# Two chained attention blocks on one core: another order for the first image, and softmax tiles handed on in halves of 512 queries

## The chip, the core and the metric

The kernel runs on one NeuronCore of a Trainium2 chip. Its engines are TensorE (PE in the profile; the loading of its weights is PEld), VectorE (DVE), ScalarE (ACT), GpSimd (POOL) and SyncE (SP), which only issues DMAs here. Each engine works through its own list of instructions in the order in which the program wrote them, and the engines meet at semaphores. The metric is the device time of one execution in microseconds (us), as the median of several runs; lower is better.

## The reference

Eight images of 256 channels by 1024 pixels pass through two attention blocks. Cut to what is computed:

```
# block 0, for each image x of [256, 1024]
q, k = Wq @ x + bq, Wk @ x + bk          # [32, 1024] each
v    = Wv @ x + bv                       # [256, 1024]
attn = softmax(q.T @ k, axis=-1)         # [1024, 1024]
x    = gamma * (v @ attn.T) + x
# block 1
h    = group_norm(x, 32 groups) * w + b
q, k, v = q_w @ h + q_b, k_w @ h + k_b, v_w @ h + v_b        # [256, 1024] each
attn = softmax(q.T @ k / 16, axis=-1)
x    = x + proj_w @ (v @ attn.T) + proj_b
```

All inputs and outputs are float32.

## The kernel before

**Precision.** Each big product is made of three matmuls. An operand is split into a rounded part (`_hi`) and the rest (`_lo`), and hi by hi, hi by lo and lo by hi are added up (lines 597 to 599). So whatever ScalarE casts into a `_hi` tile, VectorE (or GpSimd) must subtract into a `_lo` tile before the product can run.

**Block 0 of an image** has these pieces. `qk` (two halves of 512 pixels) projects queries and keys, and ScalarE and VectorE copy them out to `q4` and `k4`. `scores` (8 tiles of 128 query rows by 1024 keys, line 607) exist only for the sums of the softmax: VectorE takes the row maximum (line 1067), ScalarE takes the exponent and sums the row (line 844). After eight tiles ScalarE takes the logarithm (line 849), VectorE makes the `shift` of each query (lines 1092 to 1094), TensorE turns it into a row (line 636), and ScalarE copies that to `q4` (line 854). `keys` (8 tiles of 128 keys by 1024 queries, line 617) are the transposed scores with the shift already in them. ScalarE takes their exponent (line 820), which is the finished probability, and rounds it (line 834), VectorE subtracts (line 1084), and TensorE multiplies the tile by the values, twelve matmuls into four banks (half of the queries times half of the channels). `value0` (4 tiles) projects the values.

**Block 1** does the same with 8 `logits` tiles and its own `query` and `value1` projections. The weights of block 1 are first multiplied with each other (`weights`, line 701), and their biases too (`bias`, lines 704 to 718).

**Where results stand.** PSUM holds a `ring` of four slots of 1024 columns. While values are summed, slots 2 and 3 are theirs, and every score, keys, projection and shift tile takes turns in slots 0 and 1. TensorE may write a slot only after the engines have read what stood there before: `wait_read` looks up the reader of the former tenant. The table `PLACE` gives the slots by hand, `HOST` lets a half tile share the slot of another.

**What sets the order.** The order is written out by hand in `first_image`, `second_image` and `turn`, as a list of steps. A step has one keys or logits tile (`tile`), one tile whose values are summed (`values`, two steps behind), and lists of other entries: `early` stands right behind the tile, `sides` between the first `banks_first` banks and the others, `late` at the end. All engines walk through the same list, and each does its own part of each entry: ScalarE its exponent or copy, VectorE its maximum or subtraction. An entry moved in the list moves on all three engines.

**The first image** has nothing beside it: loads, splits, `qk`, values and scores one after the other, while the scores of image 1 (`scores 1,k`) are laced in between its keys tiles. In what follows, `keys 0,4` is the keys tile 4 of image 0, `value0 1,0` the first value tile of image 1, and so on.

## Time and profile before

| | us |
|---|---|
| median of 3 runs | 789.38 |
| lowest and highest | 786.51, 790.51 |
| profiled execution, device time | 785.61 |
| its span in the trace | 783.8 |
| TensorE busy | 774.1 (99%) |
| VectorE busy | 554.7 (71%) |
| ScalarE busy | 470.7 (60%) |
| GpSimd busy | 163.8 (21%) |

The span runs from the first to the last instruction. The mean granted clock of TensorE was 0.998 of full speed. A matmul counts as busy from its start to a modelled end, which overlaps the next one (0.39 us for 512 columns, while the next starts after 0.23). The starts are the sharper measure, and a stall shown as idle before an instruction is some 0.16 us longer when it is read from the starts.

### The profile page before, as it was taken

How to read it: one execution, taken by the hardware profiler on the slowest of the kernel's cores; microseconds unless marked ns; L12 is line 12 of the kernel's file. 1: busy time of each engine (PE TensorE's matmuls, PEld its weight loads, DVE VectorE, ACT ScalarE, POOL GpSimd, SP SyncE). 2: the span in 40 equal slices, each digit the busy share in tenths (PEclk: the TensorE clock that was granted, in tenths of full speed). 3: DMA queues.
4: the chain of work that ended last, by engine and by line, in shares of the span. 5: the costliest groups of instructions: out<-in, count | busy, mean ns of one | idle time of the engine just before them, and what ended most of it. 6: DMA issues, size and time to landing. Idle time of an engine off the chain costs nothing.

```text
span 783.8 us, 9844 instructions
## 1 busy us (share of the span) xinstructions
PE 774.1 (99%) x3816; PEld 647.4 (83%) x3816; DVE 554.7 (71%) x806; ACT 470.7 (60%) x619; POOL 163.8 (21%) x147
## 2 busy tenths in 40 slices
PE   9899999999999999999999999999999999999998
PEld 8678888888888888888888888888888888888886
DVE  5966778787578875788657796677856765476664
ACT  4876566567555775467745586456855566345343
POOL 5730052023100331005110240102310024111120
PEclk9999999999999999999999999999999999999999
DMA  6010010002000110001100011000100000000101
GB/s 189 0 55 1 1 54 1 1 23 86 1 1 1 55 54 1 1 1 54 55 1 1 0 56 54 1 1 0 54 1 2 0 33 22 1 0 1 54 1 54
DMA packets 10365, 18.98 MB, mean 24 GB/s; under 512 B 2128, under 2 KB 3920, under 8 KB 10320
## 3 DMA queue, kind: packets, MB, share of 16 engines
q1 hardware_dynamic: 10320, 18.36, 6.8%
q8 instruction: 30, 0.49, 0.3%
q14 instruction: 15, 0.12, 0.1%
HBM read 9.97 MB, written 8.39 MB: 23 GB/s over the span
## 4 chain that ended last, share of the span: by engine, by line
PE 95%; ACT 2%; DVE 2%; issue 0%; POOL 0%; ACTq 0%; DVEq 0%; POOLq 0%
PE ring L597 29%; PE ring L599 28%; PE ring L598 28%; PE ring L617 4%; PE ring L607 3%; PE ring L594 1%; ACT ring L844 1%; ACT pt_hi L834 1%; ACT prob L820 1%; PE ring L636 1%; DVE neg_max L1067 0%; DVE res L1120 0%; DVE pt_lo L1084 0%; PE ring L691 0%; PE ring L716 0%
## 5 line engine op out<-in xcount | busy, mean ns | idle before, releaser
L597 PE MATMUL ring<-pt_hi,v_hi 128*128 128x512 f32 x480 | 189.4, 395 | 0.0
L599 PE MATMUL ring<-pt_hi,v_lo 128*128 128x512 f32 x480 | 188.5, 393 | 0.0
L598 PE MATMUL ring<-pt_lo,v_hi 128*128 128x512 f32 x480 | 188.3, 392 | 0.0
L823 ACT ACTIVATE prob<-ring,neg_max 128x1024 f32<-128x1024 f32 x64 | 71.5, 1118 | 155.1 <-DVE neg_max L1070 155.1
L1069 DVE TENSOR_REDUCE neg_raw<-ring 128x1 f32<-128x1024 f32 x64 | 78.2, 1222 | 58.0 <-PE ring L599 57.9
L504 POOL TENSOR_TENSOR v_lo<-v_f,v_hi 128x512 fp32r<-128x512 f32 x28 | 37.7, 1347 | 385.1 <-ACT v_hi L861 385.1
L1084 DVE TENSOR_TENSOR pt_lo<-prob,pt_hi 128x1024 fp32r<-128x1024 f32 x64 | 81.8, 1278 | 37.5 <-ACT pt_hi L834 37.3
L599 PEld LDWEIGHTS ring<-pt_hi,v_lo 128*128 128x128 f32 x480 | 90.3, 188 | 19.9
L597 PEld LDWEIGHTS ring<-pt_hi,v_hi 128*128 128x128 f32 x480 | 90.5, 188 | 18.4 <-issue 0.4
L598 PEld LDWEIGHTS ring<-pt_lo,v_hi 128*128 128x128 f32 x480 | 90.6, 189 | 18.2
L1067 DVE TENSOR_REDUCE neg_max<-ring 128x1 f32<-128x1024 f32 x64 | 77.7, 1223 | 35.4 <-PE ring L607 35.3
L844 ACT ACTIVATE ring<-ring,neg_max 128x1024 f32<-128x1024 f32 x64 | 69.4, 1084 | 39.9 <-DVE neg_max L1067 39.8
L1087 DVE SCALAR_TENSOR_TENSOR pt_lo<-prob,row_inv,pt_hi 128x1024 fp32r<-128x1024 f32 x64 | 83.1, 1298 | 8.6 <-ACT pt_hi L837 8.4
L597 PE MATMUL ring<-h_hi,query_hi 128*128 128x512 f32 x224 | 88.0, 393 | 0.0
L598 PE MATMUL ring<-h_lo,query_hi 128*128 128x512 f32 x224 | 87.5, 391 | 0.0
L599 PE MATMUL ring<-h_hi,query_lo 128*128 128x512 f32 x224 | 87.5, 391 | 0.0
L820 ACT ACTIVATE prob<-ring 128x1024 f32<-128x1024 f32 x64 | 65.5, 1024 | 36.4 <-PE ring L617 36.2
L837 ACT ACTIVATE pt_hi<-prob,row_inv 128x1024 fp32r<-128x1024 f32 x64 | 73.7, 1152 | 9.6 <-DVE row_inv L1076 9.3
L834 ACT CAST pt_hi<-prob 128x1024 fp32r<-128x1024 f32 x64 | 67.3, 1051 | 5.3
L599 PEld LDWEIGHTS ring<-h_hi,query_lo 128*128 128x128 f32 x224 | 42.0, 188 | 8.9
L597 PEld LDWEIGHTS ring<-h_hi,query_hi 128*128 128x128 f32 x224 | 42.1, 188 | 8.8 <-ACT prob L823 0.2
L598 PEld LDWEIGHTS ring<-h_lo,query_hi 128*128 128x128 f32 x224 | 42.1, 188 | 8.6
(167 smaller groups left out, 1346.8 us busy)
## 6 DMA issues: line engine op xcount, KB each, us to landing
out_y<-res SPq DMA_DIRECT2D x32, 256.0 KB, 2.2
x_in<-in_x SPq DMA_DIRECT2D x7, 1024.0 KB, 4.9
x_in<-in_x SPq DMA_DIRECT2D x2, 512.0 KB, 5.2
h_f<-in_wv_t SPq DMA_DIRECT2D x1, 256.0 KB, 4.4
res<-in_wq SPq DMA_DIRECT2D x1, 256.0 KB, 6.8
res<-in_wk SPq DMA_DIRECT2D x1, 256.0 KB, 7.1
res<-in_wv SPq DMA_DIRECT2D x1, 256.0 KB, 7.6
res<-in_wp_t SPq DMA_DIRECT2D x1, 256.0 KB, 7.1
```

What stands on the lines that cost most here:

```text
L597: mm(out, w_hi, m_hi, start=first, stop=False)
L598: mm(out, w_hi, m_lo, start=False, stop=False)
L599: return mm(out, w_lo, m_hi, start=False, stop=last)
L820: activation(prob[:, p % PROBS], ring[:, slot], ACT.Exp).then_inc(S["keys_exp"], 1)
L823: activation(prob[:, p % PROBS], ring[:, slot], ACT.Exp, bias=neg_max[:, k % 2:k % 2 + 1], accum_out=row_sum[:, k % 2:k % 2 + 1]).then_inc ...
L834: copy(pt_hi[p % PT][:], prob[:, p % PROBS]).then_inc(S["p_hi"], 1)
L837: activation(pt_hi[p % PT][:], prob[:, p % PROBS], ACT.Identity, scale=row_inv[:, k % 2:k % 2 + 1]).then_inc(S["p_hi"], 1)
L844: activation(ring[:, slot], ring[:, slot], ACT.Exp, bias=neg_max0[:, k:k + 1], accum_out=row_sum0[:, k:k + 1]).then_inc(S["scores_exp"], 1)
L1067: V.tensor_reduce(neg_max0[:, k:k + 1], src, AX_X, ALU.max, negate=True).then_inc(S["scores_max"], 1)
L1069: link(V.tensor_reduce(neg_raw[:, k % 2:k % 2 + 1], src, AX_X, ALU.max, negate=True))
L1084: V.tensor_tensor(lo[:], src, hi[:].bitcast(F32), ALU.subtract).then_inc(S["p_split"], 1)
L1087: V.scalar_tensor_tensor(lo[:], src, row_inv[:, k % 2:k % 2 + 1], hi[:].bitcast(F32), ALU.mult, ALU.subtract).then_inc(S["p_split"], 1)
```

## The change

Only the first image, the start of image 1 and the keys tiles of all images are touched.

- **Loads.** The first half of image 0 is loaded first, in two pieces of 128 channels, and then the query and key weights. The second half and the small biases follow in exchanged order. The first splits go piece by piece: four casts of 128x512 on ScalarE and four subtractions on VectorE in place of two and two of 128x1024. TensorE's opening run of matmuls on a tile of ones is 18 long in place of 30.
- **Queries and keys of image 0.** For the second half ScalarE, not VectorE, makes the first key part, and the first four score tiles wait for the first half of the queries only.
- **Order of image 0.** Before the scores stands one value tile in place of two. Value tile 1 and the four weight products stand between the score tiles, value tiles 2 and 3 and both `qk` halves of image 1 around the shift and the first keys tiles. `scores 1,0` to `scores 1,7` move later: they stand at the end of steps 3, 4 and 5 and within steps 6, 7 and 8, where they stood right behind the keys tiles of steps 2 to 7.
- **Halves.** ScalarE makes each keys tile as exponent, cast, exponent, cast of 512 columns each, VectorE subtracts half by half, and the first two banks of the values wait for the first half only.
- **Bias products.** The same products in another order, the wide ones in pieces of 128 columns.

The core of the diff:

```diff
-PLACE = {("qk", 1, 0): 2, ("value0", 0, 2): 3, ("bias", 0, 0): 3}
+PLACE = {("qk", 0, 0): 1, ("qk", 0, 1): 0, ("value0", 0, 0): 3, ("value0", 0, 2): 0, ("qk", 1, 0): 2, ("shift", 0, 0): 1,
+         ("keys", 0, 0): 1, ("keys", 0, 1): 3, ("bias", 0, 0): 3}
+PLACE.update({("scores", 0, k): (2, 1, 0)[k % 3] for k in range(TILES)})
 PLACE.update({("keys", 0, k): 1 for k in range(2, TILES)})
-PLACE.update({("scores", 1, k): 0 for k in range(7)})
+PLACE.update({("scores", 1, k): int(k in (5, 7)) for k in range(TILES)})
 PLACE.update({("value0", 1, 0): 1, ("value0", 1, 1): 1, ("value0", 1, 2): 0})
...
-    for k in range(6):
-        steps[k + 2].early = tiles("scores", 1, (k,))
+    steps[0].late = tiles("qk", 1, (1,))
+    steps[1].late = tiles("value0", 0, (3,))
+    for k, s in enumerate((3, 4, 5)):
+        steps[s].late = tiles("scores", 1, (k,))
     steps[4].sides = tiles("value0", 1, (0,))
-    steps[6].sides = tiles("value0", 1, (1,))
+    steps[6].sides = tiles("value0", 1, (1,)) + tiles("scores", 1, (3,))
     steps[6].x_lo_end = 2, 0
-    s8, s9, s10 = Step(None, (0, 0, 6)), Step(None, (0, 0, 7)), Step(("keys", 1, 1))
+    steps[7].sides, steps[7].late = tiles("scores", 1, (4,)), tiles("scores", 1, (5,))
+    s8, s9, s10 = Step(None, (0, 0, 6), 3), Step(None, (0, 0, 7)), Step(("keys", 1, 1))
+    s8.early_behind = True
     s8.early = tiles("scores", 1, (6, 7))
...
+                    ("x0_loaded0", ((x_in[0][:, 0, half_cols[0]], x_v[0][:, 0, half_cols[0]]),)),
+                    ("x0_loaded1", ((x_in[0][:, 1, half_cols[0]], x_v[0][:, 1, half_cols[0]]),)),
                     ("wqk_loaded", ((wqk_f, by_tile(wqk_t)),)),
-                    ("x0_loaded", ((x_in[0][:, :, half_cols[0]], x_v[0][:, :, half_cols[0]]),)),
+                    ("bqk_loaded", ((bqk_s[:], bqk), (bk0_s[:], bk0))),
...
-                if 0 in banks:
-                    wait("p_split", p + 1)
                 for b in banks:
                     half, ct = bank_of[b]
+                    if layer == 0 and b == 0:
+                        wait("half_split", i * TILES + k + 1)
+                    elif b == (0 if layer else CT):
+                        wait("p_split", p + 1)
...
-            keep_busy(ring[:, 3], 30)
+            keep_busy(ring[:, 3], 18)
...
+            def keys_probs(tile):
...
+                for half, cols in enumerate(half_cols):
+                    part = prob[:, p % PROBS][:, cols]
+                    done = ("keys_half", "keys_exp")[half]
+                    activation(part, ring[:, slot][:, cols], ACT.Exp).then_inc(S[done], 1)
+                    if half == 0 and p >= PT:
+                        name, n = values_done(TILE_OF[p - PT])
+                        act.wait_ge(S[name], n)
+                    act.wait_ge(S[done], i * TILES + k + 1)
+                    copy(pt_hi[p % PT][:, cols], part).then_inc(S[("half_hi", "p_hi")[half]], 1)
```

How this moves the instructions is shown at step 4 of image 0, on two engines. TensorE before, from the keys tile on: L617 is `keys 0,4`, L607 is `scores 1,2`, L597 to L599 on `pt` are half of the values of tile 2, and L597 on `wv0` begins `value0 1,0`, whose slot `keys 0,4` held.

```order
L617 MATMUL ring<-q4_0,k4_0 128x512 [waits keys_exp]
L617 MATMUL ring<-q4_0,k4_0 128x512
L607 MATMUL ring<-k4_1,q4_1 128x512 [waits scores_exp]
L607 MATMUL ring<-k4_1,q4_1 128x512
L597 MATMUL ring<-pt_hi2,v0_hi 128x512 [waits p_split,value0_first]
L598 MATMUL ring<-pt_lo2,v0_hi 128x512
L599 MATMUL ring<-pt_hi2,v0_lo 128x512
L597 MATMUL ring<-pt_hi2,v0_hi 128x512
L598 MATMUL ring<-pt_lo2,v0_hi 128x512
L599 MATMUL ring<-pt_hi2,v0_lo 128x512
L597 MATMUL ring<-wv0_hi,h_hi 128x256 [waits keys_exp]
```

TensorE after, at the same place. L616 is the scores line there, L626 the keys line, L601 to L603 the three matmuls:

```order
L616 MATMUL ring<-k4_1,q4_1 128x512 [waits qk_split,key_hi,value0_kept]
L616 MATMUL ring<-k4_1,q4_1 128x512
L626 MATMUL ring<-q4_0,k4_0 128x512 [waits keys_exp]
L626 MATMUL ring<-q4_0,k4_0 128x512
L601 MATMUL ring<-pt_hi2,v0_hi 128x512 [waits half_split,value0_first]
L602 MATMUL ring<-pt_lo2,v0_hi 128x512
L603 MATMUL ring<-pt_hi2,v0_lo 128x512
L601 MATMUL ring<-pt_hi2,v0_hi 128x512
L602 MATMUL ring<-pt_lo2,v0_hi 128x512
L603 MATMUL ring<-pt_hi2,v0_lo 128x512
L601 MATMUL ring<-wv0_hi,h_hi 128x256 [waits keys_exp]
```

The score tile (`scores 1,0`) now stands just ahead of `keys 0,4`, not behind it, and the value tile waits for the same exponent (`keys_exp`) as before.

ScalarE before, around the same step: L820 and L834 are the exponent and the cast of a keys tile, L844 is the exponent of a score tile, L876 the cast of a value tile.

```order
L834 CAST pt_hi3<-prob 128x1024 [waits keys_exp]
L844 ACTIVATE ring,row_sum0<-ring,neg_max0 128x1024 [waits scores_max]
L820 ACTIVATE prob<-ring 128x1024 [waits ring_ready,p_split]
L834 CAST pt_hi0<-prob 128x1024 [waits keys_exp,tile_done]
L844 ACTIVATE ring,row_sum0<-ring,neg_max0 128x1024 [waits scores_max]
L876 CAST v0_hi<-ring 128x512 [waits ring_ready]
```

ScalarE after: L864 and L869 are exponent and cast of half a keys tile, L875 is the exponent of a score tile, L907 the cast of a value tile.

```order
L869 CAST pt_hi3<-prob 128x512 [waits keys_exp]
L875 ACTIVATE ring,row_sum0<-ring,neg_max0 128x1024 [waits scores_max]
L864 ACTIVATE prob<-ring 128x512 [waits ring_ready,p_split]
L869 CAST pt_hi0<-prob 128x512 [waits keys_half,tile_done]
L864 ACTIVATE prob<-ring 128x512
L869 CAST pt_hi0<-prob 128x512 [waits keys_exp]
L907 CAST v0_hi<-ring 128x512 [waits ring_ready]
```

Between the keys tiles 3 and 4 there stands one score tile's exponent in both. Before it is that of `scores 1,1`, which TensorE writes one step before `keys 0,4`, and now that of `scores 1,0`, which TensorE writes directly ahead of it.

## Rows read from the trace of the kernel before

**Rows 1.** The page: busy us, share, count; and TensorE's busy tenths in 40 slices.

```profile
PE 774.1 (99%) x3816; PEld 647.4 (83%) x3816; DVE 554.7 (71%) x806; ACT 470.7 (60%) x619; POOL 163.8 (21%) x147
...
PE   9899999999999999999999999999999999999998
```

**Rows 2.** Windows: the start-up, and the stretch at a lower granted clock.

```profile
9.12:69.03 59.91, 54.40 (x274) 43.07 (x272) 45.19 (x50) 44.12 (x64) 30.27 (x28) 1.00 0.15 49
75.70:79.10 3.40, 3.40 (x9) 2.63 (x9) 3.30 (x10) 2.23 (x3) 0.00 (x0) 0.50 0.00 0
```

**Rows 3.** Timeline of TensorE: start, length, line, names, count, idle before.

```profile
0.98 8.39 PE L594 MATMUL ring<-ones 128*128 128x128 f32 x60 [0.98 <-POOL unit L544]
9.12 0.48 PE L597 MATMUL ring<-x_hi,wqk_hi 128*128 128x512 f32 x1
...
12.01 0.28 PE L597 MATMUL ring<-wv_hi,x_hi 128*128 128x256 f32 x1
12.12 0.28 PE L598 MATMUL ring<-wv_lo,x_hi 128*128 128x256 f32 x1
...
15.74 1.62 PE L607 MATMUL ring<-k,q 96*128 96x512 f32 x6 [0.75 <-DVE q L1039]
...
28.52 0.64 PE L636 MATMUL ring<-ident_r,shift_pair 128*2 128x128 f32 x8 [0.81 <-DVE shift_pair L1094]
...
35.56 0.40 PE L597 MATMUL ring<-pt_hi,v_hi 128*128 128x512 f32 x1
35.79 0.40 PE L598 MATMUL ring<-pt_lo,v_hi 128*128 128x512 f32 x1
...
40.38 0.73 PE L607 MATMUL ring<-k,q 96*128 96x512 f32 x2 [1.46 <-ACT ring L844]
...
46.00 0.28 PE L597 MATMUL ring<-wv_hi,h_hi 128*128 128x256 f32 x1
```

**Rows 4.** Timeline of TensorE, later.

```profile
55.08 0.28 PE L597 MATMUL ring<-wv_hi,h_hi 128*128 128x256 f32 x1
...
69.03 0.65 PE L636 MATMUL ring<-ident_r,shift_pair 128*2 128x128 f32 x8
```

**Rows 5.** Timeline of VectorE, same columns.

```profile
7.06 1.22 DVE L962 TENSOR_TENSOR x_lo<-x_in,x_hi 128x1024 fp32r<-128x1024 f32 x1 [3.38 <-ACT x_hi L805]
...
14.74 0.74 DVE L1039 SCALAR_TENSOR_TENSOR q<-ring,bqk_s,q 32x512 fp32r<-32x512 f32 x1
16.48 6.88 DVE L1067 TENSOR_REDUCE neg_max<-ring 128x1 f32<-128x1024 f32 x6 [0.99 <-PE ring L607]
...
34.36 0.68 DVE L1046 TENSOR_SCALAR h_f<-ring 128x512 f32<-128x512 f32 x1
...
36.05 1.90 DVE L1084 TENSOR_TENSOR pt_lo<-prob,pt_hi 128x1024 fp32r<-128x1024 f32 x1 [0.42 <-ACT pt_hi L834]
```

**Rows 6.** Timeline of ScalarE, same columns.

```profile
5.99 1.04 ACT L805 CAST x_hi<-x_in 128x1024 fp32r<-128x1024 f32 x1 [3.98 <-DMA x_in<-in_x]
...
10.87 0.68 ACT L886 ACTIVATE q<-ring,bqk_s 64x512 fp32r<-64x512 f32 x1 [2.33 <-PE ring L599]
...
17.73 1.09 ACT L844 ACTIVATE ring<-ring,neg_max 128x1024 f32<-128x1024 f32 x1 [2.12 <-DVE neg_max L1067]
18.75 0.19 ACT L844 ACTIVATION_READ_ACCUMULATOR ring<-ring,neg_max 128x1 f32 x1
...
27.56 0.21 ACT L849 ACTIVATE log_sum<-row_sum 128x8 f32<-128x8 f32 x1
...
31.08 1.02 ACT L820 ACTIVATE prob<-ring 128x1024 f32<-128x1024 f32 x1 [0.18 <-PE ring L617]
32.14 1.04 ACT L834 CAST pt_hi<-prob 128x1024 fp32r<-128x1024 f32 x1
```

**Rows 7.** Timeline of GpSimd, same columns.

```profile
8.77 1.50 POOL L512 CAST wv_hi<-h_f 128x512 fp32r<-128x512 f32 x1 [5.77 <-DMA ident_s<-in_ident]
10.35 1.28 POOL L513 TENSOR_TENSOR wv_lo<-h_f,wv_hi 128x512 fp32r<-128x512 f32 x1
```

More of the change, by code:

```diff
@@ L706, in bias_products @@
                 value_b_ps, rowk_ps, query_b_ps = bias_places(slot)
-                for o in range(CT):
-                    mm(value_b_ps[:, 0:C], bv_rows[:, o], wp_f[:, o], start=o == 0, stop=o == CT - 1)
                 for j in range(2):
@@ L713, in bias_products @@
                 for ct in range(CT):
+                    cols = slice(ct * P, (ct + 1) * P)
+                    for o in range(CT):
+                        mm(value_b_ps[:, cols], bv_rows[:, o], wp_f[:, o, cols], start=o == 0, stop=o == CT - 1)
                     for out, w, b in ((rowk_ps, wq_f, bk_s), (query_b_ps, wk_f, bq_s)):
@@ L782, in _ @@
                 for entry in now.early + front if now.early_in_front else front + now.early:
-                    fill(entry)
+                    if not (now.early_behind and entry in now.early):
+                        fill(entry)
                 if now.values:
                     values(now.values, range(now.banks_first))
+                if now.early_behind:
+                    for entry in now.early:
+                        fill(entry)
                 for entry in now.sides:
@@ L796, in _, with first_split_x @@
             nc.scalar.preload_act_table_set("natural_log_exp_and_others")
+            def first_split_x():
+                for half in range(HALVES):
+                    for ct in range(CT):
+                        if half == 0:
+                            act.wait_ge(S[("x0_loaded0", "x0_loaded1")[ct]], 16)
+                        else:
+                            act.wait_ge(x_loaded[0], x_loads(0))
+                        copy(x_hi[:, ct, half_cols[half]], x_in[0][:, ct, half_cols[half]]).then_inc(S["x0_hi"], 1)
             def split_x(i):
+                act.wait_ge(x_loaded[i % 2], x_loads(i))
                 for half in range(HALVES):
                     cols = half_cols[half]
-                    if i == 0 and half == 0:
-                        act.wait_ge(S["x0_loaded"], 16)
-                    else:
-                        act.wait_ge(x_loaded[i % 2], x_loads(i))
                     copy(x_hi[:, :, cols], x_in[i % 2][:, :, cols]).then_inc(S["x_hi"], 1)
@@ L887, in query_part, with first_key_part @@
                            bias=bqk_s[0:64]).then_inc(S["qk_hi"], 1)
+            def first_key_part(entry):
+                act.wait_ge(S["ring_ready"], RING_NO[entry] + 1)
+                activation(k4[0][0:32, half_cols[entry[2]]], half_place(entry)[64:96], ACT.Identity,
+                           bias=bqk_s[64:96]).then_inc(S["key_first"], 1)
             def key_part(entry):
@@ L895, in opening @@
                 log_sums(0)
-                for m in range(2):
-                    query_part(("qk", 1, m))
                 shift_rows(("shift", 0, 0))
+                query_part(("qk", 1, 0))
                 key_part(("qk", 1, 0))
@@ L910, in follow @@
                     project_hi(entry)
-            split_x(0)
+            first_split_x()
             for now in STEPS:
@@ L957, in _, with first_split_x @@
             scale = C ** -0.5
+            def first_split_x(half):
+                cols = half_cols[half]
+                for ct in range(CT):
+                    dve.wait_ge(S["x0_hi"], CT * half + ct + 1)
+                    last = V.tensor_tensor(x_lo[:, ct, cols], x_in[0][:, ct, cols], x_hi[:, ct, cols].bitcast(F32),
+                                           ALU.subtract)
+                last.then_inc(S["x_split"], 1)
             def split_x(i, half):
                 cols = half_cols[half]
-                dve.wait_ge(S["x_hi"], 2 * i + half + 1)
+                dve.wait_ge(S["x_hi"], 2 * (i - 1) + half + 1)
                 V.tensor_tensor(x_lo[:, :, cols], x_in[i % 2][:, :, cols], x_hi[:, :, cols].bitcast(F32),
@@ L973, in first_weights @@
             def first_weights():
+                first_split_x(0)
                 dve.wait_ge(S["wqk_loaded"], 16)
                 split(wqk_hi[:], wqk_lo[:], wqk_f).then_inc(S["layer0_split"], 1)
-                for half in range(HALVES):
-                    split_x(0, half)
+                first_split_x(1)
             def biases(slot):
@@ L1015, in project_lo @@
                     last.then_inc(S["query_split"], 1)
+                if entry == ("value0", 0, 3):
+                    keep_values()
                 if kind == "value0" and i:
@@ L1056, in opening @@
                 shifts(0)
-                for m in range(2):
-                    key_part(("qk", 1, m))
-                for m in range(2):
-                    query_part(("qk", 1, m))
+                take_weights()
+                key_part(("qk", 1, 0))
+                query_part(("qk", 1, 0))
             def row_max(entry):
```

109 lines of the change are left out of this document (58 added, 51 removed).

## Prediction

> **What bounds the kernel now.** I read the page first. TensorE is busy for 774.1 of 783.8 us, and only the first slices and the last are not full [rows 1]. So from about 69 us on only TensorE's own work counts, and a change of order can win or lose only ahead of that. The window from the first projection to the shift of image 1 shows 54.40 busy of 59.91 us [rows 2]. Counted from the starts it is emptier: 512 columns start every 0.23 us (35.56 to 35.79) and 256 every 0.12 us [rows 3], which makes the matmuls of that window 51.1 us (24 score and keys tiles at 0.47, 4 `qk` halves and 7 value0 tiles at 1.41, 7.5 value sums at 2.73, and 3.9 for the weight products and the shift) and leaves 8.8 us of stalls. Ahead of it lie 9.12 us of start. The window at 75.70 shows a granted clock of 0.50 for 3.40 us [rows 2], 1.7 us lost. These three (9.12, 8.8, 1.7) are all that there is to win.
>
> Marks by which I compare: `value0 1,0` starts at 46.00, `value0 1,1` at 55.08 and the shift of image 1 at 69.03 [rows 3, 4]. At the third, the same work is done before and after.
>
> **Prices.** A score or keys tile takes 0.47 on TensorE and reaches its reader 0.74 after its start (15.74 to 16.48) [rows 3, 5]. A row maximum is 1.22 (1.15 each in a row), then ScalarE's exponent 1.09 plus its sum of 0.19, 1.21 until the slot is free, 1.13 for the next [rows 5, 6]. Exponent and cast of a whole keys tile start 1.06 apart and take 1.02 and 1.04 [rows 6]. No row shows a half on ScalarE. By length alone it would be 0.51; the 512-wide bias activation took 0.68 [rows 6]. I take 0.59 for each half and 0.62 and 0.53 between starts, nearer to the first since the whole tile has one such start in it: 1.74 from the first exponent to the end of the second, 2.30 for all four, where the whole tile takes about 2.05. So ScalarE gets 0.25 us more per tile, 16 us over 64 tiles, off the path: it is 60% busy. VectorE's halves cost 0.6 each (34.36: 0.68 long) [rows 5].
>
> **1. Start: about 2 us won, then 0.** Before, the first projection starts at 9.12, when the run of ones ends (0.98 + 8.39) [rows 3], though the first `x_lo` is ready at 7.06 + 1.22 = 8.28 [rows 5]. Now 18 passes are over at about 6.4. The same 640 KB have to land, which they had by 5.99 [rows 6]; then the weight split (about 0.75) comes last, so the projection starts at 7.2. Its second half waits for casts and subtractions of the second load (two of each, until about 9.55) and ends at 11.1. But `value0 0,0` needs GpSimd's split of its weights, which ended at 10.35 + 1.28 = 11.63 [rows 7] and whose load is now issued one place later: 12.0, as before (12.01). The lead is gone there. It comes back because one value tile, not two, stands ahead of the scores: TensorE reaches them at 13.4, VectorE ends its last query part at 14.36 (15.48 before) and takes the first maximum at 14.4, not 16.48.
>
> **2. Scores of image 0: a lead of 2.1 us.** Eight exponents at 1.13 and one copy of 0.59 (`value0 0,1`, now among them) follow from 15.65: the last ends at 25.4, the logarithm starts at 25.45 (27.56 before [rows 6]), the shift on TensorE at 26.4 (28.52). The weight products and one value tile fit into TensorE's waits.
>
> **3. From the shift to the first values: the lead is spent.** Before, the `qk` halves of image 1 were done by the shift. Now ScalarE idles 1.5 us for the shift (26.4 + 0.68 = 27.1), copies it until 28.1, waits for `qk 1,0`, copies that (two at 0.71) and starts `keys 0,0` at 30.1 (31.08 before [rows 6]). Behind it stand `qk 1,1` (1.42) and two more tiles (4.6): their last cast starts at 37.9 and ends at 38.5, about where before (38.0). The value banks take the slot of the `qk` tiles of image 1, whose last query part VectorE ends at 35.45: values start at 35.65, before at 35.56 [rows 3]. There `scores 1,0` was done, now it isn't. The next tile has no stall, where 40.38 showed 1.46 (1.62 by starts) [rows 3]. Net: `scores 1,0` at 41.6, `keys 0,4` at 42.05, half of values 2 until 43.9. Before, that point was 46.00 with two score tiles more done (0.94): 1.2 us ahead.
>
> **4. `value0 1,0`: what decides.** It takes the slot of `keys 0,4`, so it waits for that tile's exponent, before and now. What changed is what ScalarE has in front: the exponent of `scores 1,0`, which TensorE writes directly ahead. From `scores 1,0` at 41.6: 0.74 to the maximum, 1.25 to the exponent, 1.13 to `keys 0,4`, 1.74 to its end: 46.5. TensorE is there at 43.9 and stands 2.6 us. All engines work in list order, so nothing can pass. Before, the score tile was written a step earlier.
>
> **5. `value0 1,1`: again, longer.** `scores 1,1` starts at 46.5 + 1.41 + 1.37 = 49.3. Then 0.74, 1.25, 1.13: `keys 0,5` on ScalarE at 52.4, its last cast done 2.39 later (54.8). VectorE must subtract that before it takes the maximum of `scores 1,2` (0.65: 55.45). Then 1.25 and 1.13, `keys 0,6` at 57.8, and 1.74: 59.6. TensorE's own work from 49.3 is only 6.0 us (two score and two keys tiles, one and a half value sums), so 4.4 us are lost, 0.8 ahead of `keys 0,6` and 3.6 ahead of `value0 1,1`, which starts at 59.6, not 55.08 [rows 4], with three score tiles done, not five.
>
> **6. Until the shift.** Five score tiles are left where there were three. `scores 1,3` to `1,7` stand between 61.0 and 72.0; VectorE's subtraction of `keys 0,7` (until 68.0) is ahead of the maximum of `scores 1,4`, and the last four go one by one through maximum and exponent: TensorE waits 0.35, 1.05, 0.55 and 0.35. Log at 74.85, shift at 75.8 against 69.03 [rows 4].
>
> **Sum.** 7.2 of start + 51.1 of work + stalls of 1.1 and 0.9 (start), 2.5 (scores), 0.6 (shift), 3.0 (first values), 2.6, 0.8, 3.6 and 2.3 = 75.7 to 75.8; before 9.12 + 51.1 + 8.8 = 69.0. So +6.8. Behind it TensorE is full, the halves have room, and I leave the lower clock as it is. The profiled execution took 785.61 us: 792.4. It lies 3.8 under the median of 789.38, so on the scale of the medians 796.2, which I give as 796.
>
> **Bounds.** Ten halves stand on the chains of 4 and 5: at 0.51 each they give 0.8 back, at 0.68 they cost 0.9. The start may be 0.6 off either way by the loads. VectorE and GpSimd: a subtraction of 1.22 elsewhere took 1.90 [rows 5] while GpSimd worked; GpSimd now works for the values 2 and 3 while `keys 0,3` is subtracted, 0 to 0.7 more. The reordered bias products hold the same 24 one-column matmuls, in a row before. The lower clock stands right behind them [rows 2]; it may stay (0), go (-1.7), or also follow the new stalls (+1.7 each).
>
> The Trainium skill, "TensorE: Matmul & The Clock Gate", section "HAM oscillation — how this bites in real kernels", says that idle gaps between bursts of matmuls drop the engine to half clock. The trace agrees that it is not only a full stop that counts (0.50 at 75.70, behind narrow matmuls without a gap [rows 2]), yet the 1.46 us at 40.38 brought none. By that rule the stalls of 2.6 and 3.6 us would cost up to 1.7 us each, and the sum would be 795.8 on the profile's scale in place of 792.4.
>
> **Rivals.**
> - *The clock falls at the new stalls*, by the mechanism just priced: half speed for as long as at 75.70, behind one or both: +8.5 to +10.2, 798 to 800. For it: 3.6 us is over twice any stall now. Against: it needs TensorE to be the bound just then. 0.15.
> - *Smaller stalls, no measurable change.* Halves at 0.51 (-0.8), a start 0.6 sooner, the lower clock gone (-1.7): +3.7, 793. 0.17.
> - *Faster.* ScalarE's exponent of `scores 1,k` is not in the way, because the keys exponent gets free earlier than I read: the place is `value0 1,0`, and it decides if the exponent of `keys 0,4` ends before 43.9. Then the 1.2 us lead stands, the two chains cost nothing, and with the lower clock gone it is -1.2 - 1.7: 786.5; if ScalarE's idle time of section 3 is avoided too, 2 us more: 784.5. For it: the lead of 2.1 at the shift. Against: the list order leaves no way round. 0.10.
> - *The forecast*, +5 to +8: 0.58.
>
> A change under 0.5% (3.9 us) can't be told from none. Slower 0.72, same 0.19, faster 0.09. The range of 788 to 801 leaves out the faster rival (about 1 in 10) and little at the top, since it holds the lower clock at both stalls.
>
> **What would show it.** Right: TensorE idle 2 to 3 us ahead of `value0 1,0` and 3 to 4 ahead of `value0 1,1`, both released by ScalarE's exponent of a keys tile; shift of image 0 near 26.4 and of image 1 near 75.8; nothing new behind that. Wrong: no idle of over 1.5 us at those two tiles, or a first value sum well ahead of 35, which would mean that section 3 spends less than I think, or stalls in later images, which would mean that ScalarE's extra 16 us have no room.

## The result

The changed kernel takes 813.24 us (811.13 to 815.18, four runs), the kernel before 788.64 us (786.51 to 790.51, four runs; the table ahead of the prediction has 789.38 from three of them). The ratio is 1.0312, with a 95% interval of 1.0274 to 1.035: 3.1% slower. The forecast was 796 with a range of 788 to 801. The direction was right and the size was not: +24.6 us between the medians, +27.4 us of span in the profiled executions (783.8 to 811.2), where +6.8 was forecast.

### The profile page after: what moved, and what is told of

Same layout as the page of the kernel before. It is cut to its first block, busy times and chain, and to the rows that moved or that the text cites. A ratio compares the mean times of both kernels' runs of the same rounds, so it can differ in the third digit from the quotient of the medians.

```text
span 811.2 us, 10013 instructions
## 1 busy us (share of the span) xinstructions
PE 788.2 (97%) x3796; PEld 650.8 (80%) x3796; DVE 564.6 (70%) x871; ACT 488.5 (60%) x750; POOL 161.4 (20%) x147
## 4 chain that ended last, share of the span: by engine, by line
PE 80%; ACT 12%; DVE 4%; issue 2%; DMA 1%; SPq 0%; ACTq 0%; DVEq 0%
PE ring L601 26%; PE ring L603 24%; PE ring L602 24%; ACT prob L864 5%; ACT pt_hi L869 4%; PE ring L626 3%; PE ring L616 2%; ACT h_hi L832 1%; DVE neg_max L1119 1%; ACT ring L875 1%; DMA x_in<-in_x 1%; PE ring L645 0%; DVE pt_lo L1140 0%; DVE h_lo L1016 0%; PE ring L710 0%
## 5 line engine op out<-in xcount | busy, mean ns | idle before, releaser
L601 PE MATMUL ring<-pt_hi,v_hi 128*128 128x512 f32 x480 | 190.6, 397 | 2.9 <-DVE q L1092 2.9
L603 PE MATMUL ring<-pt_hi,v_lo 128*128 128x512 f32 x480 | 189.4, 395 | 0.0
L1140 DVE TENSOR_TENSOR pt_lo<-prob,pt_hi 128x512 fp32r<-128x512 f32 x128 | 91.8, 734 | 36.1 <-ACT pt_hi L869 35.6
L601 PEld LDWEIGHTS ring<-pt_hi,v_hi 128*128 128x128 f32 x480 | 91.3, 190 | 22.0 <-issue 3.7
L603 PEld LDWEIGHTS ring<-pt_hi,v_lo 128*128 128x128 f32 x480 | 91.0, 190 | 20.0
L875 ACT ACTIVATE ring<-ring,neg_max 128x1024 f32<-128x1024 f32 x64 | 69.5, 1086 | 49.7 <-DVE neg_max L1119 49.6
L864 ACT ACTIVATE prob<-ring 128x512 f32<-128x512 f32 x128 | 75.9, 593 | 32.1 <-PE ring L626 31.4
L601 PE MATMUL ring<-h_hi,query_hi 128*128 128x512 f32 x224 | 88.0, 393 | 0.0
L603 PE MATMUL ring<-h_hi,query_lo 128*128 128x512 f32 x224 | 87.5, 391 | 0.0
L869 ACT CAST pt_hi<-prob 128x512 fp32r<-128x512 f32 x128 | 79.5, 621 | 7.4
L603 PEld LDWEIGHTS ring<-h_hi,query_lo 128*128 128x128 f32 x224 | 42.1, 188 | 8.9
L601 PEld LDWEIGHTS ring<-h_hi,query_hi 128*128 128x128 f32 x224 | 42.1, 188 | 8.9 <-DVE v_lo L1067 0.2
```

Source lines behind the costliest of these rows:

```text
L601: mm(out, w_hi, m_hi, start=first, stop=False)
L603: return mm(out, w_lo, m_hi, start=False, stop=last)
L864: activation(part, ring[:, slot][:, cols], ACT.Exp).then_inc(S[done], 1)
L869: copy(pt_hi[p % PT][:, cols], part).then_inc(S[("half_hi", "p_hi")[half]], 1)
L875: activation(ring[:, slot], ring[:, slot], ACT.Exp, bias=neg_max0[:, k:k + 1], accum_out=row_sum0[:, k:k + 1]).then_inc(S["scores_exp"], 1)
L1140: V.tensor_tensor(lo[:, cols], src[:, cols], hi[:, cols].bitcast(F32), ALU.subtract).then_inc(S[("half_split", "p_split")[half]], 1)
```

## The profile after

The page: busy us, share of the span and count; TensorE's busy tenths and the granted clock in 40 slices; the new groups of half keys tiles (exponent, cast, subtraction: busy, mean ns of one, idle before).

```profile
PE 788.2 (97%) x3796; PEld 650.8 (80%) x3796; DVE 564.6 (70%) x871; ACT 488.5 (60%) x750; POOL 161.4 (20%) x147
...
PE   8887999999999999999999999999999999999998
...
PEclk9899899999999999999999999999999999999999
...
L864 ACT ACTIVATE prob<-ring 128x512 f32<-128x512 f32 x128 | 75.9, 593 | 32.1 <-PE ring L626 31.4
L869 ACT CAST pt_hi<-prob 128x512 fp32r<-128x512 f32 x128 | 79.5, 621 | 7.4
L1140 DVE TENSOR_TENSOR pt_lo<-prob,pt_hi 128x512 fp32r<-128x512 f32 x128 | 91.8, 734 | 36.1 <-ACT pt_hi L869 35.6
```

ScalarE has 17.8 us more than in [rows 1], about the 16 that were forecast, and is still at 60%. TensorE has 14 us more of busy time in 20 fewer instructions. Part of that is a lower clock: the mean granted clock fell from 0.998 to 0.987. It is not a matter of one execution: the four runs show 0.983 to 0.989, and no run of the kernel before in the experiments below shows less than 0.993.

TensorE's timeline at the marks of the prediction (start, length, line, names, count, idle before):

```profile
0.98 7.15 PE L598 MATMUL ring<-ones 128*128 128x128 f32 x36 [0.98 <-POOL unit L547]
7.88 0.48 PE L601 MATMUL ring<-x_hi,wqk_hi 128*128 128x512 f32 x1
...
14.19 1.87 PE L616 MATMUL ring<-k,q 96*128 96x512 f32 x6
...
28.64 0.64 PE L645 MATMUL ring<-ident_r,shift_pair 128*2 128x128 f32 x8 [0.36 <-DVE shift_pair L1152]
...
37.88 0.77 PE L601 MATMUL ring<-pt_hi,v_hi 128*128 128x512 f32 x1 [2.93 <-DVE q L1092]
...
50.30 0.39 PE L601 MATMUL ring<-wv_hi,h_hi 128*128 128x256 f32 x1 [2.40 <-ACT prob L864]
...
59.63 0.73 PE L626 MATMUL ring<-q,k 98*128 98x512 f32 x2 [0.57 <-ACT prob L864]
...
65.07 0.58 PE L601 MATMUL ring<-wv_hi,h_hi 128*128 128x256 f32 x1 [3.33 <-ACT prob L864]
...
82.56 0.64 PE L645 MATMUL ring<-ident_r,shift_pair 128*2 128x128 f32 x8
...
86.09 1.20 PE L626 MATMUL ring<-q,k 98*128 98x512 f32 x4 [1.44 <-DVE v_lo L1067]
```

Read the brackets first. The long stalls that were forecast are there with their size, once the 0.16 us are added by which a bracket is short of the starts: 2.40 ahead of `value0 1,0` (2.6 forecast), 0.57 and 3.33 ahead of `keys 0,6` and `value0 1,1` (0.8 and 3.6). Yet the marks run away from the forecast ones, and the windows show why (columns: us, then busy of TensorE, weight load, VectorE, ScalarE, GpSimd with counts, granted clock, DMA share, GB/s):

```profile
9.12:82.56 73.44, 60.16 (x266) 47.01 (x265) 45.88 (x58) 46.99 (x82) 28.89 (x28) 0.91 0.13 45
20.66:24.07 3.41, 3.41 (x9) 2.67 (x9) 2.12 (x3) 3.14 (x6) 3.25 (x5) 0.50 0.02 5
37.73:41.14 3.41, 3.26 (x8) 2.62 (x9) 3.41 (x5) 2.79 (x5) 0.92 (x1) 0.50 0.00 0
51.40:54.80 3.40, 3.40 (x13) 2.82 (x12) 0.92 (x2) 0.59 (x1) 1.51 (x2) 0.50 0.36 142
65.05:68.45 3.40, 3.38 (x14) 3.28 (x15) 0.89 (x2) 1.04 (x2) 0.00 (x0) 0.50 0.00 0
88.92:95.75 6.83, 6.83 (x26) 6.06 (x26) 4.03 (x12) 4.86 (x9) 0.00 (x0) 0.50 0.00 0
```

Four stretches at half clock ahead of the shift of image 1 where there was none [rows 2], and one of 6.83 us after it in place of 3.40. The first of the four can't be put down to the change. Three kernels below keep the old order of image 0 (halves alone, exponents first on the kernel before, bias products), and the profile of each has such a stretch at 22 to 23 us and its shift of image 0 at 30.6 to 30.8, not at 28.52; that of the kernel before happens to have none. The one of halves alone, same columns:

```profile
23.17:26.58 3.41, 3.41 (x15) 3.12 (x14) 1.57 (x3) 2.44 (x6) 0.00 (x0) 0.50 0.00 0
```

| mark | forecast | measured | late by | stretch in between |
|---|---|---|---|---|
| first projection | 7.2 | 7.88 | 0.7 | the run of ones lasts 7.15, not about 5.4 |
| first scores | 13.4 | 14.19 | 0.8 | |
| shift of image 0 | 26.4 | 28.64 | 2.2 | 20.66 |
| first values | 35.65 | 37.88 | 2.2 | |
| `value0 1,0` | 46.5 | 50.30 | 3.8 | 37.73 |
| `value0 1,1` | 59.6 | 65.07 | 5.5 | 51.40 |
| shift of image 1 | 75.8 | 82.56 | 6.8 | 65.05 |

From mark to mark with a stretch in between, the lateness grows by 1.3 to 1.7 us. In all that makes +13.5 us up to the shift of image 1 (82.56 against 69.03 [rows 4]), and 13.9 are still missing. The weight loads of TensorE show where most of them are. Waits of the weight load (engine, line, releaser: us in total, times, longest) from 100 to 700 us, the kernel before:

```profile
PEld ring L597 <- issue: 0.4, 1, 0.4
PEld ring L597 <- ACT prob L823: 0.2, 1, 0.2
```

and the changed one:

```profile
PEld ring L601 <- ACT prob L864: 13.4, 25, 0.6
PEld ring L601 <- DVE v_lo L1067: 2.0, 2, 1.8
```

Twenty-five times TensorE waits for the exponent of a keys tile: five times in each of five images, ahead of two query, two `value1` and one `qk` projection. One of them in the timeline of all engines, same columns as above:

```profile
209.26 0.60 ACT L864 ACTIVATE prob<-ring 128x512 f32<-128x512 f32 x1 [1.21 <-PE ring L626]
...
209.95 0.62 ACT L869 CAST pt_hi<-prob 128x512 fp32r<-128x512 f32 x1
...
210.48 0.59 ACT L864 ACTIVATE prob<-ring 128x512 f32<-128x512 f32 x1
210.60 0.39 PE L603 MATMUL ring<-pt_hi,v_lo 128*128 128x512 f32 x1
...
211.12 0.19 PEld L601 LDWEIGHTS ring<-h_hi,wqq_hi 128*128 128x128 f32 x1 [0.55 <-ACT prob L864]
211.12 0.50 PE L601 MATMUL ring<-h_hi,wqq_hi 128*128 128x512 f32 x1
```

The same place in the kernel before:

```profile
190.26 1.03 ACT L820 ACTIVATE prob<-ring 128x1024 f32<-128x1024 f32 x1 [1.22 <-PE ring L617]
...
191.62 0.39 PE L599 MATMUL ring<-pt_hi,v_lo 128*128 128x512 f32 x1
191.63 0.19 PEld L597 LDWEIGHTS ring<-h_hi,wqq_hi 128*128 128x128 f32 x1
191.85 0.40 PE L597 MATMUL ring<-h_hi,wqq_hi 128*128 128x512 f32 x1
```

The query projection takes the slot of a keys tile, and has to wait for the end of its exponent. Before, that slot was free 1.03 us after the exponent's start (191.29), 0.34 ahead of the weight load at 191.63. (In the trace of before this room is 0.34 at the 20 places with query and `value1` projections and 0.62 at the five with `qk`.) Now the cast of the first half stands between the two exponents, the slot is free after 1.81 (210.48 + 0.59), and TensorE's next matmul starts 0.52 after the last one (210.60 to 211.12) where 0.23 is the usual step: some 0.3 lost here. (The bracket of 0.55 counts from the end of the last weight load.) Add up, over the starts of all matmuls from 100 to 700 us, what goes beyond 0.23 us behind 512 columns, 0.12 behind 256 or 258 and 0.06 behind fewer: it grows from 6.1 to 17.2 us. Of these 11.1 us some 8 lie in the 25 places, 0.33 at each with the step behind it, and 1.5 at one wait of a query projection for VectorE:

```profile
126.54 0.50 PE L601 MATMUL ring<-h_hi,wqq_hi 128*128 128x512 f32 x1 [1.31 <-DVE v_lo L1067]
```

The sum: 13.5 up to the shift of image 1, 1.4 ahead of `keys 1,0` at 86.09, 1.7 for the longer half clock at 88.92, 11.1 in the later images: 27.7 where 27.4 was measured.

## Experiments

Two theories for the cost behind the shift: **slot** (the second exponent of each keys tile ends later, so its slot is given back later) and, as its rival, **load** (ScalarE and VectorE have 18 and 10 us more to do). For the first image: **order** (the score tiles of image 1 stand in the wrong place) and **clock** (the new stalls bring the half clock). Runs of one round share the runs of the kernel before: 786.84, 787.06 and 786.91 us.

### Whole tiles

The changed kernel, with each keys tile as one exponent, one cast, one subtraction again (ScalarE's part; VectorE's subtraction and the waits are put back too).

```diff
-                for half, cols in enumerate(half_cols):
...
-                    activation(part, ring[:, slot][:, cols], ACT.Exp).then_inc(S[done], 1)
...
-                    copy(pt_hi[p % PT][:, cols], part).then_inc(S[("half_hi", "p_hi")[half]], 1)
+                activation(prob[:, p % PROBS], ring[:, slot], ACT.Exp).then_inc(S["keys_exp"], 1)
...
+                copy(pt_hi[p % PT][:], prob[:, p % PROBS]).then_inc(S["p_hi"], 1)
```

> The changed kernel with whole keys tiles again: one exponent, one cast, one subtraction of 1024 columns, the values wait for the whole tile. Theory A (the second half's exponent frees the tile's slot about 0.7 us later than the whole exponent did, which stops TensorE some 25 times for 0.4 us in the later images, about 10 us): 799 to 803 us against 813.2, and TensorE stands nowhere behind 130 us. Theory B (the later images are slower because of the new slots or of the state in which the first image leaves them): 811 to 814. Both: the stalls ahead of value0 1,0 and value0 1,1 stay, 0.7 us shorter each.

Measured: 801.63 us, ratio 1.0182 [1.0153, 1.0212]. The 25 waits are gone, and the loss by starts from 100 to 700 us is 7.9. The stalls of the first image stay, though not both 0.7 shorter, as was expected: one has gone from 2.40 to 1.76, the other from 3.33 to 3.59.

```profile
48.33 0.38 PE L601 MATMUL ring<-wv_hi,h_hi 128*128 128x256 f32 x1 [1.76 <-ACT prob L859]
...
61.04 0.58 PE L601 MATMUL ring<-wv_hi,h_hi 128*128 128x256 f32 x1 [3.59 <-ACT prob L859]
```

So all of the change but the halves costs 14.8 us, and the long stall ahead of `value0 1,1` does not come from the halves. Part of the 14.8 is clock. This profile has 17.1 us of half clock, some 8.5 us lost, where that of the kernel before has 3.4 and 1.7. Two of its three stretches:

```profile
60.77:64.18 3.41, 3.14 (x13) 3.06 (x14) 1.22 (x1) 1.44 (x3) 0.00 (x0) 0.50 0.00 0
84.66:94.90 10.24, 10.24 (x42) 9.47 (x42) 5.74 (x11) 4.68 (x5) 0.00 (x0) 0.50 0.00 0
```

The first goes with the stall of 3.59. Behind the stall of 1.76 no half clock was granted.

### Halves alone

The same edit the other way: the kernel before, with halves.

```diff
-                    activation(prob[:, p % PROBS], ring[:, slot], ACT.Exp).then_inc(S["keys_exp"], 1)
+                    for half, cols in enumerate(half_cols):
...
+                        activation(part, ring[:, slot][:, cols], ACT.Exp).then_inc(S[done], 1)
...
+                        copy(pt_hi[p % PT][:, cols], part).then_inc(S[("half_hi", "p_hi")[half]], 1)
...
-                    copy(pt_hi[p % PT][:], prob[:, p % PROBS]).then_inc(S["p_hi"], 1)
```

> The kernel before with the halves alone: exponent, cast, exponent, cast, two subtractions, the first two banks wait for the first half. Theory A: 798 to 800 us (788.6 and about 10), with the stalls ahead of query, value1 and qk tiles of later images. Theory B: 788 to 790.

Measured: 799.41 us, 1.0146 [1.0117, 1.0176]. Its shift of image 1 comes at 73.05, 4.0 later than before. Of that 2.3 are there at the shift of image 0 (30.82), behind the half clock from 23.17. The run of the bias products meets that too, without any halves (30.80). The weight load shows the row of the changed kernel again:

```profile
PEld ring L597 <- ACT prob L825: 13.4, 25, 0.6
```

### Halves in another order

The changed kernel, with exponent, exponent, cast, cast in place of exponent, cast, exponent, cast. The number of operations and their lengths are the same, so this one tells slot from load.

```diff
                 for half, cols in enumerate(half_cols):
...
-                    copy(pt_hi[p % PT][:, cols], part).then_inc(S[("half_hi", "p_hi")[half]], 1)
+                    activation(prob[:, p % PROBS][:, cols], ring[:, slot][:, cols],
+                               ACT.Exp).then_inc(S[("keys_half", "keys_exp")[half]], 1)
...
+                for half, cols in enumerate(half_cols):
...
+                    copy(pt_hi[p % PT][:, cols],
+                         prob[:, p % PROBS][:, cols]).then_inc(S[("half_hi", "p_hi")[half]], 1)
```

> The changed kernel, ScalarE's four half operations in the order exponent, exponent, cast, cast, so as many operations as in the changed kernel, but the slot is free 0.6 us sooner. Theory A: 802 to 805 us, the recurring stalls are gone or under 0.1 us. Theory C (what costs in the later images is ScalarE's 0.25 us more per tile, its fixed cost): 812 to 814, nothing changes.

Measured: 799.58 us, 1.016 [1.0129, 1.019], some 2 us under what was expected. The loss by starts from 100 to 700 us is back at 6.7, against 6.1 in the kernel before, and the wait of 1.31 at 126.54 is gone too. ScalarE's timeline at the place shown above:

```profile
209.46 1.09 ACT L862 ACTIVATE prob<-ring 128x512 f32<-128x512 f32 x2 [1.22 <-PE ring L626]
210.44 1.14 ACT L869 CAST pt_hi<-prob 128x512 fp32r<-128x512 f32 x2
```

The slot is free 1.09 after the start, not 1.81. The edit also moves the wait for the buffer of the cast behind both exponents, but at the place shown above the first cast began 0.09 after its exponent, so it waited for nothing. With ScalarE's and VectorE's extra work in place, almost the whole cost in the later images is gone: load is refuted, slot is shown. The two long stalls of the first image stay (2.65 and 3.44).

The same order of halves (the + side of this diff) on the kernel before, with nothing else changed:

> The kernel before with halves in the order exponent, exponent, cast, cast. By theory A (slot release) the 25 recurring stalls of the other order of halves don't appear: 786 to 788 us, within 0.3% of before. If ScalarE's extra 0.25 us per tile costs something by itself: 790 or more.

Measured: 788.42 us (12 runs) against 787.06, 1.0017 [1.0, 1.0033]. The halves as such are almost free, and bring nothing.

### Scores where they were

The changed kernel, with `scores 1,k` right behind the keys tiles of steps 2 to 7 again (cut; the parts come in another order than in the kernel).

```diff
-    for k, s in enumerate((3, 4, 5)):
-        steps[s].late = tiles("scores", 1, (k,))
+    for k in range(6):
+        steps[k + 2].early = tiles("scores", 1, (k,))
...
-    s8, s9, s10 = Step(None, (0, 0, 6), 3), Step(None, (0, 0, 7)), Step(("keys", 1, 1))
-    s8.early_behind = True
+    s8, s9, s10 = Step(None, (0, 0, 6)), Step(None, (0, 0, 7)), Step(("keys", 1, 1))
...
-    s9.sides = tiles("value0", 1, (2,)) + tiles("shift", 1, (0,))
+    s8.late = tiles("value0", 1, (2,))
+    s9.sides = tiles("shift", 1, (0,))
...
-PLACE.update({("scores", 1, k): int(k in (5, 7)) for k in range(TILES)})
+PLACE.update({("scores", 1, k): 0 for k in range(7)})
```

Steps 8 and 9 are put back as well, with `value0 1,2` in step 8.

> The changed kernel, halves included, with the scores of image 1 where they stood before (right behind the keys tiles of steps 2 to 7, in slot 0). Theory A: the stalls of 2.4 and 3.3 us ahead of value0 1,0 and 1,1 shrink to under 1 us, and at least three of the six stretches at half clock go: 799 to 803 us. Theory D (the loss in the first 90 us lies in the new order of image 0 itself, loads, weight products and qk): above 806.

Measured: 801.96 us, 1.0185 [1.0154, 1.0215]. Both stalls ahead of value0 tiles are gone, and the shift of image 1 comes at 72.66. In their place stands one that I had not counted:

```profile
37.66 1.19 PE L615 MATMUL ring<-k,q 96*128 96x512 f32 x2 [5.32 <-DVE x L1105]
```

`scores 1,0` takes slot 0, which `value0 0,2` holds until VectorE has copied it, and VectorE does that after the subtraction of a keys tile. So the scores could not simply stay where they were: value tiles 2 and 3 had been moved ahead of them. The 25 waits of the halves are there too (13.3, 25 times).

Both undone in the changed kernel (the diffs of the first and of this experiment together):

> The changed kernel with both suspects undone: whole tiles, and the scores of image 1 where they stood before. If the two losses add up (halves about 12 us, score order about 12 us), this is within 3 us of before: 787 to 790, with the one stall of about 5 us ahead of scores 1,0 that the run with the early scores showed. If a third part of the change costs by itself (loads, order of image 0): above 792.

Measured: 789.49 us, 1.004 [1.0022, 1.0058], with the same stall (5.4). Against the kernel before: halves alone +12.6, the rest of the change alone +14.8, both +26.4 (813.24 against 786.84, not of one round), the new loads and the new start of image 0 with neither +2.6.

### The bias products

The kernel before with the new order of the bias products, since the half clock stands right behind them.

```diff
-                for o in range(CT):
-                    mm(value_b_ps[:, 0:C], bv_rows[:, o], wp_f[:, o], start=o == 0, stop=o == CT - 1)
...
+                    cols = slice(ct * P, (ct + 1) * P)
+                    for o in range(CT):
+                        mm(value_b_ps[:, cols], bv_rows[:, o], wp_f[:, o, cols], start=o == 0, stop=o == CT - 1)
```

> The kernel before with the bias products alone in the order of the changed kernel. If the new order keeps the clock up, the stretch at half clock at about 75 us goes and the time falls by up to 1.7 us (785.1 against 786.8). If the order is nothing to the clock: the stretch stays behind the bias products in most executions, no change. If it makes it worse: one or two stretches, up to 1.7 us slower.

Measured: 787.27 us (10 runs), 1.0005 [0.9985, 1.0025]. Half clock is still granted for 3.4 us there, from 77.7. So this part of the change shows no effect on the time. The stretch is no fixed price of these products: the profiles of both kernels with halves and the old order of image 0 have the old products and full clock there (1.00 in both from 70 to 85 us).

### The stalls filled

The changed kernel, with six passes over the tile of ones ahead of `value0 1,0` and of `value0 1,1`, once the exponent of the score tile is done. TensorE would have stood there anyway.

```diff
                 before = BEFORE[entry]
+                if entry in (("value0", 1, 0), ("value0", 1, 1)):
+                    wait("scores_exp", TILES + 1 + 2 * m)
+                    keep_busy(ring[:, 0], 6)
```

> The changed kernel, and in the two long stalls (ahead of value0 1,0 and 1,1) TensorE runs 6 passes on the tile of ones (1.3 us each time) once the exponent of the score tile in slot 0 is read, so that the stalls stay as long but TensorE idles 1.3 us less in each. If the idle time in them is what lowers the clock (51 and 65 us): those two stretches go and the kernel gets 2 to 3.4 us faster than 813.2, 810 to 811. If the clock falls for another cause: 813 to 814 and stretches at half clock at the same places.

Measured: 812.67 us, 1.032 [1.0293, 1.0347]: no gain that can be told from none. Two windows, same columns as above:

```profile
9.12:80.16 71.04, 60.55 (x290) 47.09 (x289) 46.88 (x58) 46.65 (x81) 28.95 (x28) 0.95 0.13 43
85.40:95.60 10.20, 10.20 (x42) 9.43 (x42) 5.96 (x14) 6.09 (x11) 0.00 (x0) 0.50 0.00 0
```

The stretches at 51.40 and 65.05 are gone (0.95 in place of 0.91), and the shift of image 1 comes 2.4 us sooner, at 80.16. That these two stretches come from the stalls does not rest on this one execution. In the three profiles that have the stalls, half clock began at most 0.3 us ahead of and 1.1 us behind the end of each one of 2.40, 2.65, 3.33, 3.44 and 3.59 us (changed kernel, exponents first, whole tiles), and not at the one of 1.76 or at the two filled ones. But the stretch at the bias products is now 10.20 long, 1.7 us more lost, and so the total missed the expectation. Nothing shows that the filling made it longer: with whole tiles, and nothing filled, it is 10.24 long.

### Towards a better kernel

**Mixed.** The changed kernel with the exponents first, `scores 1,0` to `1,4` right behind the keys tiles of steps 3 to 7, and `1,5` late in step 7.

```diff
-    for k, s in enumerate((3, 4, 5)):
-        steps[s].late = tiles("scores", 1, (k,))
+    for k in range(5):
+        steps[k + 3].early = tiles("scores", 1, (k,))
...
-    steps[6].sides = tiles("value0", 1, (1,)) + tiles("scores", 1, (3,))
+    steps[6].sides = tiles("value0", 1, (1,))
...
-    steps[7].sides, steps[7].late = tiles("scores", 1, (4,)), tiles("scores", 1, (5,))
+    steps[7].late = tiles("scores", 1, (5,))
```

> The changed kernel's order of image 0, halves in the order exponent, exponent, cast, cast, and scores 1,0 to 1,4 right behind the keys tiles of steps 3 to 7 (scores 1,5 to 1,7 as in the changed kernel). By my theory no long stall ahead of value0 1,0 and 1,1 (under 0.5 us), no recurring ones, and of the lead at the shift of image 0 (28.64 against 28.52 in the changed kernel with a clock fall, 26.4 without) something is kept: 785 to 790 us. If the new order of image 0 costs by itself: above 793.

Measured: 790.95 us (784.77 to 792.24, 12 runs), 1.0031 [1.001, 1.0053], just above the range that was expected. The profiled execution was one of the two fastest (784.85, granted clock 0.999) and had full clock from 7.1 to 781 us. It is not the usual one: seven of the twelve runs show 0.988 to 0.991 and took 790.8 to 792.2 us.

```profile
26.66 0.64 PE L645 MATMUL ring<-ident_r,shift_pair 128*2 128x128 f32 x8 [0.41 <-DVE shift_pair L1153]
...
35.82 0.47 PE L601 MATMUL ring<-pt_hi,v_hi 128*128 128x512 f32 x1 [2.85 <-DVE q L1093]
```

```profile
9.12:68.28 59.16, 53.62 (x266) 42.00 (x266) 46.61 (x58) 45.21 (x82) 31.66 (x28) 1.00 0.15 53
```

This is the test of the prediction's ledger at full clock, up to the first values, where the two kernels have the same order: its 26.4 and 35.65 are measured as 26.66 and 35.82. It also shows a stall of 2.85 us with no half clock behind it, and a shift of image 1 at 68.28, 0.75 ahead of the kernel before.

**Opened.** The same, with both `qk` halves of image 1 copied ahead of `keys 0,0`, `scores 1,5` in the sides of step 7 and `value0 1,2` late in step 8.

```diff
-    opening.late = tiles("shift", 0, (0,)) + tiles("qk", 1, (0,))
+    opening.late = tiles("shift", 0, (0,)) + tiles("qk", 1, (0, 1))
...
-    steps[0].late = tiles("qk", 1, (1,))
...
-    steps[7].late = tiles("scores", 1, (5,))
-    s8, s9, s10 = Step(None, (0, 0, 6), 3), Step(None, (0, 0, 7)), Step(("keys", 1, 1))
+    steps[7].sides = tiles("scores", 1, (5,))
+    s8, s9, s10 = Step(None, (0, 0, 6)), Step(None, (0, 0, 7)), Step(("keys", 1, 1))
...
-    s9.sides = tiles("value0", 1, (2,)) + tiles("shift", 1, (0,))
+    s8.late = tiles("value0", 1, (2,))
+    s9.sides = tiles("shift", 1, (0,))
```

> The mixed version again (order of image 0 as changed, halves as exponent, exponent, cast, cast, scores 1,0 to 1,4 behind their keys tiles), and both qk halves of image 1 copied out before the first keys tile's cast is subtracted, scores 1,5 within step 7, value0 1,2 at the end of step 8. The stalls of 2.9 us ahead of the first value sum and of 1.4 us ahead of keys 1,0 shrink by 1.5 us and 1.4 us: 783 to 787 us, faster than before by 0.3% or nothing. If the clock decides (it fell in some executions of the mixed version): two groups of times, as in 784.8 and 791.

Measured: 785.67 us (782.75 to 788.21, 12 runs), 0.9985 [0.9969, 1.0001]. The stall of 2.85 ahead of the first values has become one of 0.7, and the one of 1.4 ahead of `keys 1,0` one of 0.2. In this profile there is a new one at the start, where the second half of the projection waits for its splits:

```profile
PE ring L601 <- DVE x_lo L1003: 2.8, 1, 2.8
```

**Thirty passes.** The same with 30 opening passes in place of 18.

```diff
-            keep_busy(ring[:, 3], 18)
+            keep_busy(ring[:, 3], 30)
```

> The same with the opening run of 30 passes, not 18. If TensorE's idle time between the opening run and the first projections is what lets the clock fall later in the first 25 us: fewer slow executions and a narrower spread than m3_open, median at or under it. If not: the same spread, and up to 1 us slower for the later start.

Measured: 785.77 us (783.48 to 788.11, 12 runs), 0.998 [0.9962, 0.9998]. The 30 passes make no difference that can be told from none (785.67 with 18). The spread is 4.6 us against 5.5, and the times still lie in two groups, six of 783.5 to 784.2 with a clock of 1.0 and six of 787.3 to 788.1 with 0.993 to 0.995, so what was hoped of the clock is not shown. The stalls of 2 us and more are gone, as the largest waits of TensorE show:

```profile
PE ring L616 <- ACT ring L876: 1.8, 4, 0.6
PE ring L598 <- POOL unit L547: 1.0, 1, 1.0
PE ring L601 <- DVE pt_lo L1143: 0.7, 1, 0.7
```

It is the only variant whose interval lies below 1, by 0.2%, which is next to nothing, and it lies 27 us under the changed kernel.

## Why the prediction was wrong

**Start (1): right in kind.** The run of ones lasted 7.15, not about 5.4, so the projection began at 7.88 and not 7.2. Full clock was granted only from about 7.0 us on in that execution, so 18 passes took longer than I counted. (In the kernel before it was from 4.0 on.) By 12.54 GpSimd's split of the weights set the end, as forecast, though at 12.0.

**Scores of image 0 and first values (2, 3): right at full clock.** The lead of 2.1 us at the shift was there in the mixed kernel (26.66) and was spent by the first values, as forecast. In the changed kernel half clock from 20.66, between the weight products, made TensorE late for two maxima and took the lead before the shift (28.64). The kernels with the old order of image 0 lose 2.1 to 2.3 us the same way in their profiles, so against them the lead was there. I read the marks of before from an execution without this stretch, and did not ask how other executions look.

**`value0 1,0`, `value0 1,1` (4, 5): right.** Place, releaser and size, 2.56 and 0.73 + 3.49 by the starts against 2.6 and 0.8 + 3.6. The half lengths taken between the bounds (0.59, 0.62) are those measured. With whole tiles the stalls are 1.76 and 3.59: they are of the order, and the halves have only a part in the first. And with the scores moved back they give way to 5.32 us elsewhere, which the prediction had no need to see but a repair had.

**Until the shift (6): in kind.** Of the four waits that were forecast (2.3 us) two are there, 0.79 and 0.40 at 77.21 and 78.34, 1.5 us by the starts.

**Clock: the first failed step.** "I leave the lower clock as it is" was wrong by four stretches ahead of the shift (5 to 6 us of the 6.8 by which the marks are late) and 1.7 at the bias products. Some 3 us of it are the two behind the long stalls, which follow the idle time, as the stalls of five sizes and the fill run show. The rival had that mechanism at 0.15 and +1.7 each, with the right price and too little chance: the stall of 1.46 at 40.38, which brought no half clock [rows 3], was no evidence about stalls of 2.4 to 3.3. I had read the Trainium skill, "TensorE: Matmul & The Clock Gate", section "HAM oscillation — how this bites in real kernels", for the rule that idle gaps between bursts drop the engine to half clock. The trace agrees in kind, with 0.50 behind gaps of 2.40 and 3.33 us, though both are shorter than the gaps that the page warns of. The rule alone doesn't cover this kernel: at 20.66 the windows show TensorE busy for all of 3.41 us, and the mixed kernel stood for 2.85 us at full clock.

**Behind the shift: the step that failed most.** "Behind it TensorE is full, the halves have room" was a term of 0, and it measured 11.1 us in the later images. Another 1.4 at `keys 1,0` are of the order, since they are there with whole tiles too and shrink to 0.2 where `value0 1,2` stands in step 8. The term rested on the first paragraph, where TensorE's busy share was taken to mean that from 69 us on only its own work counts. I asked whether ScalarE had time for more work. It had: the experiment with the exponents first keeps the extra work and loses 0.6 us. The question was when the second exponent ends, because it gives the slot back. The halves move that from 1.03 to 1.81 us after the start, by 0.78, and the room was 0.34 at 20 places and 0.62 at five. Both numbers could be worked out before: the prediction's own prices have 1.74 from the first exponent to the end of the second, where the whole tile has 1.02, and the room stands in the trace of before, at each place where TensorE fills the slot of a keys tile. I did so for the first image, where I followed the slots, and not for the other seven. The prediction named the sign of it ("stalls in later images"), but with the wrong reason (ScalarE's 16 us).

What stays open: what decides, from one execution to the next, whether half clock is granted at about 20 us and at the stall ahead of the first values. That stall has half clock with it in three profiles (2.93, 3.17 and 2.94 us: changed kernel, whole tiles, fill) and none in two (2.86 and 2.85: exponents first, mixed), with the same work up to there but for the halves. Nor is it known what sets the length of the stretch at the bias products.

## What to carry to other kernels

Cutting an operation in two on an engine with time to spare costs that engine little and may still cost whoever waits for its *last* piece: for each resource that the operation frees, compare the new moment of release with the room that the trace shows at the next user, in every stage, not just where the order changed. Put the pieces that release the scarce buffer first (exponent, exponent, cast, cast). Where TensorE is the bound, price a new stall with half clock behind it (1.7 us each here, at five of five stalls of 2.40 us and more ahead of value tiles), look at the granted clock of several executions, and read a ledger of starts against one at full clock.

## What the runs showed of the hardware

- Half clock also stands where TensorE did not stop: 20.66 to 24.07 is 3.41 us busy of 3.41 at 0.50.
- The same kernel does not meet it in every execution. The mixed kernel's profile has none from 7.1 to 781 us, and its runs spread over 7.5 us, from 784.77 at a mean clock of 0.999 to 792.24 at 0.989; the kernel before spreads over 5 us, from 785.67 at 0.998 to 790.59 at 0.994 (29 runs).
- Stalls ahead of value tiles of 2.40 to 3.59 us had half clock with them in five cases of five, one of 1.76 us and two that were filled with passes over the tile of ones had none. The whole kernel was not measurably faster for the filling (812.67 against 813.24 us).
- A half-width exponent took 0.59 against 1.03 and a half-width cast 0.62 against 1.05: some 0.17 us per instruction do not shrink with the columns.
